# A two-layer vision kernel in fp32: y in halves, and an MLP step in another order with half-width products

## The reference

```python
# layer 0
h = depthwise_conv7x7(x) + conv_b                    # 24 channels, each by itself
h = (h - mean_c(h)) * rsqrt(var_c(h) + 1e-5) * ln_g + ln_b
h = gelu(h @ w1 + b1)                                # 24 -> 96
x = (h @ w2 + b2) * layer_scale + x                  # 96 -> 24
# layer 1
y = fc1(x) * s + t                                   # 24 -> 24
nodes = y in windows of 8 x 8                        # 64 nodes of 24 channels
idx = 9 nearest neighbours by the distance of the normalised nodes
feat = concat(node, neighbour - node)                # 9 x 48
h = max over the 9 of gelu(affine(feat @ ew))        # 48 outputs
out = affine(fc2(h)) + x
```

## Time and profile before

| | us |
|---|---|
| median of 3 runs | 2242.76 |
| lowest, highest | 2237.08, 2244.7 |
| profiled execution, its own time | 2235.85 |
| its span | 2233.8 |
| TensorE busy | 1990.3 (89%) |
| VectorE busy | 1525.1 (68%) |
| ScalarE busy | 1115.5 (50%) |
| GpSimd busy | 642.8 (29%) |
| mean granted clock of TensorE, share of 2.4 GHz | 0.934 |

### The profile page before, as it was taken

How to read it: one execution, slowest core, us unless ns; L and a number is a source line. 1 busy time by engine, 2 the same in 40 slices (tenths; PEclk the granted TensorE clock), 3 DMA queues, 4 the chain that set the end, 5 groups by cost and what they waited for, 6 DMA issues and landing times.

```text
span 2233.8 us, 45679 instructions
## 1 busy us (share of the span) xinstructions
PE 1990.3 (89%) x13970; PEld 1041.8 (47%) x13970; DVE 1525.1 (68%) x5840; ACT 1115.5 (50%) x2630; POOL 642.8 (29%) x407
## 2 busy tenths in 40 slices
PE   6998999999789888889888988888888898989986
PEld 2444555555344444444444444444444444544442
DVE  4222222222188888888788888888888797888887
ACT  0102444344356655555555555555555565655563
POOL 3002444444122222222222222322222232222232
PEclk9997999999799999999999999999899999999899
DMA  7872333333210111111111111111111111111110
GB/s 143 148 145 62 82 78 77 76 77 78 55 20 14 34 30 33 32 33 32 33 32 33 32 33 33 33 32 33 32 33 32 30 29 28 30 25 27 29 35 16
DMA packets 225814, 105.49 MB, mean 47 GB/s; under 512 B 195904, under 2 KB 222784, under 8 KB 225472
## 3 DMA queue, kind: packets, MB, share of 16 engines
q1 hardware_dynamic: 225600, 102.63, 21.8%
HBM read 54.40 MB, written 28.90 MB: 37 GB/s over the span
## 4 chain that ended last, share of the span: by engine, by line
PE 54%; issue 19%; ACT 13%; DVE 8%; POOL 5%; SPq 1%; DMA 1%; POOLq 0%; ACTq 0%; DVEq 0%
PE bank L1059 9%; PE bank L867 7%; PE bank L924 6%; PE bank L918 6%; PE bank L992 5%; ACT xam L496 4%; PE bank L1014 4%; DVE red L783 4%; PE bank L1030 3%; PE bank L892 3%; PE bank L962 2%; POOL hq L369 2%; ACT pb L512 2%; PE bank L901 2%; PE bank L955 2%
## 5 line engine op out<-in xcount | busy, mean ns | idle before, releaser
L783 DVE TENSOR_REDUCE red<-bank 128x64 f32<-128x512 f32 x1176 | 751.8, 680 | 163.8 <-PE bank L1059 145.8
L512 ACT CAST pb<-bank 64x192 bf16<-64x192 f32 x1176 | 367.3, 312 | 375.4 <-PE bank L1030 360.4
L1059 PE MATMUL bank<-onehot,pb 128*32 128x512 bf16 x7056 | 533.2, 408 | 18.5 <-issue 16.7
L369 POOL TENSOR_TENSOR hq<-red,arena 128x384 f32<-128x384 f32 x196 | 200.9, 1025 | 554.6 <-DVE red L783 539.3
L350 POOL TENSOR_TENSOR rs<-ve,mhalf 112x16 f32<-112x16 f32 x56 | 162.4, 2899 | 377.8 <-DVE ve L689 377.8
L770 DVE TENSOR_SCALAR onehot<-slot 128x256 bf16<-128x256 bf16 x1568 | 252.9, 231 | 0.0
L1059 PEld LDWEIGHTS bank<-onehot,pb 128*32 128x32 bf16 x7056 | 137.9, 98 | 207.9 <-issue 104.1
L1001 PE MATMUL bank<-arena,wqs 128*128 128x448 f32 x336 | 171.8, 595 | 42.3 <-DMA arena<-yb 38.6
L1014 PE MATMUL bank<-xb,xam 128*128 128x64 f32 x1568 | 205.8, 277 | 0.0
L1014 PEld LDWEIGHTS bank<-xb,xam 128*128 128x128 f32 x1568 | 201.8, 201 | 2.8 <-issue 2.5
L361 POOL TENSOR_TENSOR rn<-nv,mhalf 128x28 f32<-128x28 f32 x28 | 134.5, 4805 | 229.3 <-DVE nv L742 229.3
(11 more groups left out here) (92 smaller groups left out, 2719.7 us busy)
## 6 DMA issues: line engine op xcount, KB each, us to landing
arena<-yb SPq DMA_DIRECT2D x336, 56.0 KB, 2.1
arena<-in_x SPq DMA_DIRECT2D x24, 392.0 KB
ht<-conv_d SPq DMA_DIRECT2D x112, 84.0 KB
xt<-in_x SPq DMA_DIRECT2D x112, 84.0 KB
x_d<-x1o SPq DMA_DIRECT2D x112, 84.0 KB
ht<-x_d SPq DMA_DIRECT2D x112, 84.0 KB
xt<-x_d SPq DMA_DIRECT2D x56, 168.0 KB, 3.2
out<-x1o SPq DMA_DIRECT2D x112, 84.0 KB, 2.0
```

The lines of the kernel that those rows point to most:

```text
L369: nc.gpsimd.tensor_tensor(hq[:, :, :, :], red[:, k, :, :, :], qs[:, b, :, wx, :].unsqueeze(1).broadcast_to([128, 2, T, NN]), ALU.add).then ...
L512: last = nc.scalar.copy(pb[64 * u:64 * u + 64, k, part, :, :, u, :], src[64 * u:64 * u + 64, :, :, :])
L783: nc.vector.tensor_reduce(red[:, k, h, t, :], src, axis=mybir.AxisListType.X, op=op).then_inc(s["red_done"], 1)
L1059: last = mm(bank[32 * q:32 * q + 32, (k + t) % 2, :], pb[:, k, part, g, c, :, :].rearrange("p u o -> p (u o)"), onehot[:, k, g, :, :].rear ...
```

## The change

In the MLP stage:

- `variance` uses blocks of 128 pixels instead of 112, each in two halves of 64 columns of weights, 8 products instead of 4. `turn_std` follows (three blocks of 128 and one of 64). `LB` is also the partition count of `ve`, `rs` and `rse`.
- `expand` does the middle hidden block first, in two halves of output columns over all rows, and then the first and the last block in quarters of the array: rows 0 to 63 for the first, 64 to 127 for the last, each in two halves of columns. That is 6 products instead of 3.
- `contract` gives the middle block in two halves of output columns, then the first block to the lower half only and the last to the upper half only, 4 products instead of 3.
- TensorE's order for step m becomes turn_std(m+1), centre(m+4), variance(m+3), contract(m-1), expand(m). Centre is one step further ahead, and `square` on ScalarE with it, now waiting for the variance before it. gelu takes the blocks in the order middle, first, last. SyncE's and VectorE's orders stay.

In the graph stage:

- `yb` is ordered u, window, node. `load_y2` reads 448 contiguous values for each partition. `project` becomes two products, one for each half of the weights' columns.
- `fc1` of half 0 moves from window 6 to the second half of window 5, that of half 1 to the first half of window 6. `make_y` is split in two within window 6, and `square_y` comes at the end of window 6 instead of in window 0 of the next iteration. `norms` is later in VectorE's window 0, and the last `halfsq` stands before `project`.

```diff
...
 NBLK = 4
-LB = L // NBLK
+LB = 128
 NU = NI * WX
...
         outs = x1o[:, :, :].rearrange("p (b u) l -> p b u l", b=2)
-        yb = sb("yb", [128, 2, WX, 2, NN])
+        yb = sb("yb", [128, 2, 2, WX, NN])
         xa = sb("xa", [128, 2, WX, 2, NN])
...
                         g, u = (t, 3)[blk // 2], blk % 2
-                        sp.dma_start(y2[32 * blk:32 * blk + 32, b, t, :, :], yb[32 * g:32 * g + 32, b, :, u, :]
+                        sp.dma_start(y2[32 * blk:32 * blk + 32, b, t, :, :], yb[32 * g:32 * g + 32, b, u, :, :]
                                      ).then_inc(y2_in[b], 16)
             def load_res(i, b):
...
                 pool.wait_ge(s["rnt_done"], 2 * i + (k + 1))
-                nc.gpsimd.tensor_tensor(xa[:, b, lo:hi, :, :].rearrange("p w u i -> p (w u i)"),
-                                        rnt[:, lo:hi, :, :].rearrange("p w u i -> p (w u i)"),
-                                        yb[:, b, lo:hi, :, :].rearrange("p w u i -> p (w u i)"), ALU.mult
+                nc.gpsimd.tensor_tensor(xa[:, b, lo:hi, :, :], rnt[:, lo:hi, :, :],
+                                        yb[:, b, :, lo:hi, :].rearrange("p u w i -> p w u i"), ALU.mult
                                         ).then_inc(s["xa_done"], 1)
             def add_x(i, b, old, gp):
...
             def square(m, r):
                 act.wait_ge(ctr_d, m + 1)
+                at_least(act, var_d, m)
                 nc.scalar.activation(sq[:, :], bank[:, 0, 0:L], ACT.Square).then_inc(sq_d, 1)
...
             def gelu(m, r):
-                for t in range(3):
-                    act.wait_ge(mm1_d, 3 * m + (t + 1))
+                for t in (1, 0, 2):
+                    act.wait_ge(mm1_d, 3 * m + (1 if t == 1 else 3))
                     nc.scalar.activation(gl[:, t, :], bank[:, 3 + t, 0:L], ACT.Gelu, bias=b1s[:, t:t + 1], scale=1.0
...
             act.wait_ge(zeroed, 2)
-            for m in range(3):
+            for m in range(4):
                 square(m, m)
             for m in range(NBUF):
-                square(m + 3, m + 3)
+                square(m + 4, m + 4)
                 gelu(m, m)
...
                 for r in range(NBUF):
-                    square(NBUF * j + (r + 3), r + 3)
+                    square(NBUF * j + (r + 4), r + 4)
                     gelu(NBUF * j + r, r)
-            def make_y(i, b, banks=(6, 7)):
-                for u in range(2):
+            def make_y(i, b, us=(0, 1), banks=(6, 7)):
+                for u in us:
                     act.wait_ge(s["fc1_mm"], 2 * i + (u + 1))
-                    nc.scalar.activation(yb[:, b, :, u, :], bank[:, banks[u], 0:L].rearrange("p (w i) -> p w i", w=WX),
-                                         ACT.Identity, bias=c1[:, 0:1],
+                    nc.scalar.activation(yb[:, b, u, :, :].rearrange("p w i -> p (w i)"), bank[:, banks[u], 0:L], ACT.Identity, bias=c1[:, 0:1],
                                          scale=P("s1")).then_inc(s["y_done"], 1)
             def square_y(i, b):
                 act.wait_ge(s["y_done"], 2 * (i + 1))
-                nc.scalar.activation(sq2[:, :], yb[:, b, :, :, :].rearrange("p w u i -> p (w u i)"), ACT.Square
+                nc.scalar.activation(sq2[:, :].rearrange("p (w u i) -> p u w i", w=WX, u=2), yb[:, b, :, :, :], ACT.Square
                                      ).then_inc(s["ysq_done"], 1)
             def square_xa(i, b):
...
                     split(n + 1, (r + 1) % 2, 0, s["p_mm"], s["hi_done"])
-                if pre and wx == 0:
-                    square_y(i + 1, (b + 1) % 2)
+                if early and wx == 6:
+                    make_y(i + 2, b, us=(0,))
                 if ahead1:
...
                     split(n + 1, (r + 1) % 2, 2, s["res2_mm"], s["lo_done"])
+                if early and wx == 6:
+                    make_y(i + 2, b, us=(1,))
                 if pre and wx == 2:
...
                 if early and wx == 6:
-                    make_y(i + 2, b)
+                    square_y(i + 2, b)
             for m in range(NSTEP - NBUF, NSTEP):
-                if m + 3 < NSTEP:
-                    square(m + 3, m + 3)
                 gelu(m, m)
...
                     best(n - 2, r % 2, i - (wx < 2), (wx - 2) % WX, ((r - 2) % (2 * WX)) // WX, first)
-                if pre and wx == 0:
-                    norms(i + 1)
                 if pre and wx == 1:
...
                         dve.wait_ge(s["t8_done"], G * (n + 4))
+                if pre and wx == 0:
+                    norms(i + 1)
                 if gather:
...
                 for k in range(NBLK):
-                    last = mm(bank[0:LB, 2, G * k:G * k + G], sq[:, LB * k:LB * k + LB], P("mean4"), start=True, stop=True)
+                    for half in range(2):
+                        a = min(LB * k + 64 * half, L - 64)
+                        last = mm(bank[64 * half:64 * half + 64, 2, G * k:G * k + G], sq[:, a:a + 64], P("mean4"),
+                                  start=True, stop=True)
                 last.then_inc(var_d, 1)
             def turn_std(m, r):
...
                 for k in range(NBLK):
-                    last = nc.tensor.transpose(bank[:, 1, LB * k:LB * k + LB],
-                                               rse[:, r % 2, k, :, :].rearrange("p g c -> p (g c)"),
-                                               P("ident")[0:LB, 0:LB])
+                    size = min(LB, L - LB * k)
+                    last = nc.tensor.transpose(bank[:, 1, LB * k:LB * k + size],
+                                               rse[0:size, r % 2, k, :, :].rearrange("p g c -> p (g c)"),
+                                               P("ident")[0:size, 0:size])
                 last.then_inc(rb_d, 1)
             def expand(m, r):
                 pe.wait_ge(hn_d, m + 1)
-                for t in range(3):
-                    at_least(pe, gelu_d, 3 * (m - 1) + (t + 1))
-                    mm(bank[:, 3 + t, 0:L], w1g[:, t, :], hn[:, r % 2, :], start=True, stop=True).then_inc(mm1_d, 1)
+                for c in range(2):
+                    last = mm(bank[64 * c:64 * c + 64, 4, 0:L], w1g[:, 1, 64 * c:64 * c + 64], hn[:, r % 2, :],
+                              start=True, stop=True)
+                last.then_inc(mm1_d, 1)
+                for k, t in ((0, 0), (64, 2)):
+                    for c in range(2):
+                        last = mm(bank[64 * c:64 * c + 64, 3 + t, 0:L], w1g[k:k + 64, t, 64 * c:64 * c + 64],
+                                  hn[k:k + 64, r % 2, :], start=True, stop=True)
+                last.then_inc(mm1_d, 2)
             def contract(m, r):
                 at_least(pe, x1_dn, m - 1)
-                for t in range(3):
-                    pe.wait_ge(gelu_d, 3 * m + (t + 1))
-                    last = mm(bank[:, 6 + r % 2, 0:L], w2s[:, t, :], gl[:, t, :], start=t == 0, stop=t == 2)
+                for half, t in ((0, 1), (1, 1), (0, 0), (1, 2)):
+                    pe.wait_ge(gelu_d, 3 * m + (1 if t == 1 else 3))
+                    last = mm(bank[64 * half:64 * half + 64, 6 + r % 2, 0:L], w2s[:, t, 64 * half:64 * half + 64],
+                              gl[:, t, :], start=t == 1, stop=t != 1)
                 last.then_inc(mm2_d, 1)
             def mlp_slot(m, r, j, first=False):
...
                 now = m if isinstance(m, int) else 0
+                if now + 1 < end:
+                    turn_std(m + 1, r + 1)
+                if now + 4 < end:
+                    centre(m + 4, r + 4, j + (r + 4) // NBUF)
+                if now + 3 < end:
+                    variance(m + 3)
                 if not first:
                     contract(m - 1, r - 1)
-                if now + 3 < end:
-                    centre(m + 3, r + 3, j + (r + 3) // NBUF)
                 expand(m, r)
-                if now + 1 < end:
-                    turn_std(m + 1, r + 1)
-                if now + 3 < end:
-                    variance(m + 3)
...
                 variance(m)
+            centre(3, 3, 0)
             turn_std(0, 0)
...
                 at_least(pe, s["lo_done"], n)
-                both = yb[:, b, wx, :, :].rearrange("p u i -> p (u i)")
-                mm(bank[:, 3, 0:G * O], both, wp[:, :], start=True, stop=False, skip_group_check=True
-                   ).then_inc(s["p_mm"], 1)
+                for u in range(2):
+                    last = mm(bank[64 * u:64 * u + 64, 3, 0:G * O], yb[:, b, u, wx, :], wp[:, :], start=True, stop=False,
+                              skip_group_check=True)
+                last.then_inc(s["p_mm"], 1)
             def subtract(n, k, part, waits, done):
...
                 if early and wx == 6:
-                    fc1(i + 2, b, j + 1, 0)
+                    fc1(i + 2, b, j + 1, 1)
                 for e in qa:
...
                     fc2(i - 1, bn, 1)
-                if early and wx == 6:
-                    fc1(i + 2, b, j + 1, 1)
+                if early and wx == 5:
+                    fc1(i + 2, b, j + 1, 0)
```

(4 more changed lines are left out.)

## The result

The changed kernel takes 2338.64 us (median of 4 runs, 2335.68 to 2346.61) against 2241.01 for the kernel before in the same comparison: ratio 1.0442, 95% interval 1.0409 to 1.0474. The forecast was 2324, slower. The last residual of the MLP starts at 677.5 us instead of 577.1, so that stage ends 100.4 us later (forecast +100). From the end of that residual to the end of the span it is 1655.5 us instead of 1656.0 (forecast -14).

What follows compares the result with a forecast made beforehand. TensorE bounds the MLP, a TensorE-VectorE chain the graph stage; after the change SyncE's queue gates the MLP. MLP +100 (70 - 6 + 36) and graph stage -14 give +86, so 2324 us, range 2255 to 2385.

Steps and rivals of the forecast that it cites:

- Part 2: MLP stage: late ht loads in SyncE's queue make centre wait some 4 us in 24 rounds; +70 us.
- Part 3: MLP stage: waits at centre lower TensorE's clock, costing 1.5 us a round (ends 0 and 2.7), +36 us.
- Part 1: MLP step, TensorE's work: half-width products bring it from 6.65 to 5.9 us, variance at 0.85, contract at 1.7.
- case that passes start in the order written: MLP step on TensorE: contract 5u (1.9 us), expand 7 to 8u, step 6.6 to 6.7 us; u, a pass, 0.375 us.
- +100 in the MLP: MLP stage in all: +70 us for late ht loads, -6 for the other 8 steps, +36 for the low clock.
- Part 4: Graph stage, y in halves: y2 lands some 4 us sooner, its wait goes, -45 us; whole stage -14 us.
- +0.16 forecast: Graph stage, project: half-width products cost one pass more, +0.16 us to its successor (ends 0 and +0.42).
- project's 22 us: Graph stage: project's extra 0.16 us in five of seven windows, times 28, gives +22 us.
- Gate without the clock: Rival: centre waits for ht in the MLP but the clock holds; +50 us, 2289 us; chance 0.21.
- The loads keep ahead: Rival: ht comes in time, TensorE bounds the MLP at 5.9 us a step; -42 us there, 2184 us; chance 0.11.
- No overlap in fp32: Rival: halves do not overlap in the MLP, step 9.7 us, TensorE-bound; +171 us, 2397 us; chance 0.06.

Runs made afterwards that it cites:

- kept-warm run: Changed kernel plus 18 idle bf16 products of 448 columns ahead of every centre that waits for ht; 2320.5 us, ratio 1.0363.
- run with eight: Changed kernel with the MLP's old order and y2 loaded by 8 DMAs instead of 12; 2128.8 us, ratio 0.9513.
- both mended kernels: Changed kernel with ht issued ahead of the store (2188.0 us), and changed kernel with TensorE's and ScalarE's old MLP order (2172.7 us).

## Why the prediction was right, and where it was not

**The gate (Part 2), right.** The wait stands at centre, 24 times, and the loop is the one that was summed. The queue's terms held: 0.88, 8.33 (8.35), landing 2.90 (2.76). Moving the load of ht ahead in SyncE's order took it away.

**The clock (Part 3), right in kind, too small.** I took 1.5 us a round between ends of 0 and 2.7; the kept-warm run puts it at 2.6. The upper end was too low by its own rows: 0.9 for centre, 0.8 for variance and another 1.7 for a contract of twice the length are 3.4. It was not passed, as variance cost 0.4 us more and not 0.8, and centre 0.7 and not 0.9. The three products on the loop ran wholly at the low level, 5.9 us against 3.4.

**TensorE's work (Part 1), taken too dear.** The sum for the case that passes start in the order written was also wrong: with contract at 5u and expand at 7 to 8u the step is 6.7 to 7.1 us and not 6.6 to 6.7. Variance 0.49 and not 0.85; contract 1.53 and not 1.7. Eight passes in 1.53 us are 4.1 u, so halves run side by side, both passes of each, which is the 2x of the Trainium skill's "TensorEngine Tiling", Theoretical Speedup. My reading of the Trainium skill's "TensorE: Matmul & The Clock Gate", Part 3, that strict program order makes the second half wait for the first pass of its neighbour, would give 1.87 and was wrong. The drain that the Trainium skill's "TensorEngine Tiling", Key Properties, names costs at most 0.1 to 0.2 us here: the halves of expand take 0.86 and the quarters 0.91 where two whole passes take 0.75.

**+100 in the MLP, in part luck.** The round at the full clock was forecast at 16.2 and came at 15.4, of which variance and contract are 0.5; the clock was taken 1.1 too small; so 17.7 was forecast and 18.05 came. In the whole stage the gate without the clock cost +40 where +64 was forecast (MLP end of the kept-warm run), and the clock +60 where +36 was. The two errors of 24 us cancel, and that the sum fits to 0.4 us is chance. The parts, and that both are there, are not.

**y2 (Part 4), wrong.** The step that failed: "An issue takes 0.61 us now, and the store of x1, whose rows are 1792 bytes, 0.31", so that twelve, which take 8.34 us now, would take "about 4". Rows became 1792 bytes and the issue 0.59. The run with eight shows that three times the data costs 0.03 us more: among these DMAs the issue goes by their number and not by what they move. I compared DMAs that differ in more than their rows (24 partitions into DRAM against 32 partitions within SBUF). Which of these makes 0.31 or 0.59 is open; the load of x1 from DRAM, to 24 partitions too, takes 0.30, so whether DRAM is read or written is not it. The value of the wait was near: taking all but 2.3 us of it away gave 41 us (2172.7 to 2131.5), where I had put 45.

**The rest of the graph stage.** The wait of norm for square_y went as forecast (7.0 us over 15 times before, none after). In the kernel after, project starts 0.85 us behind node_terms (two passes, 0.75 before) and the gather 0.48 behind project (0.42 before), in the timeline:

```profile
1107.46 0.92 PE L1012 MATMUL bank<-arena,wqs 128*128 128x448 f32 x2
1108.31 0.55 PE L1035 MATMUL bank<-wp,yb 128*64 128x192 f32 x4
1108.79 0.83 PE L1071 MATMUL bank<-onehot,pb 128*32 128x512 bf16 x12
```

That is the +0.16 forecast, 0.10 and 0.06, but as a term of the sum it is nothing: windows 2, 3 and 4, over both iterations of a pair, last 46.4 us before and after. fc1 costs window 5 0.91 us (0.75 forecast) and gives back nothing in window 6. With y2's 45 us missing, the sum should have been about +40; it is -0.5 or, alone, -4 to -6. Besides project's 22 us, what is missing lies in window 0, which the forecast left alone but for norm. Behind the stall at the turn of TensorE's loop (once in two iterations) it lasts 11.7 us before and 9.9 after on the mean of eleven, and in the other iteration 8.6 and 8.0: some 34 us in all, 7 of them norm's. Two of the first kind before, and two after:

```profile
1192.94:1204.27 11.33, 9.52 (x68) 5.78 (x69) 5.06 (x25) 3.71 (x10) 3.84 (x1) 0.70 0.62 120
1308.91:1321.02 12.11, 10.21 (x68) 5.85 (x69) 5.05 (x24) 3.76 (x10) 3.95 (x1) 0.63 0.60 119
...
1290.83:1300.25 9.42, 9.19 (x70) 5.65 (x71) 4.20 (x19) 3.10 (x9) 3.84 (x1) 0.64 0.52 127
1406.38:1413.27 6.89, 6.38 (x70) 4.04 (x71) 4.83 (x23) 3.04 (x9) 2.94 (x1) 1.00 0.58 141
```

Most of this gain is a stall. The kernel before has two with no cause shown in each round, 23.3 us and 16.7 us over 11 times each, and the second lies in this window; the changed kernel has the first alone, 34.7 us over 11 times. It is also the window that takes the 50 us when the code is moved. So the gain, like that loss, can come from the code's place; no run tells it from the edits of the graph stage.

**The rivals.** "Gate without the clock" is the kept-warm run, and its +64 is above. "The loads keep ahead" did not happen, but it is what both mended kernels are: MLP -57, where it said -42. "No overlap in fp32" is excluded by contract's 1.53 us.

## What to carry to other kernels

When work is moved ahead by a step, look at every in-order queue that feeds it: here four DMAs stood behind a store that waits for the end of the chain which they start, and that ring, 12 us of queue and landing and 6 of products behind them, set the pace. A cheaper product pays only where its engine ends the wait last; take apart what is cheaper from what is moved, as here one gave -3.3% and the other more than took it back. A DMA's issue has a price of its own (0.59 us, and 0.62 for three times the data), so count DMAs before bytes.

## What the hardware showed that I had not expected

- The same loop on TensorE, with 54 products more ahead of it, takes 50 us more in 1656, and 44 in a second kernel, where the products stand within the MLP's code; almost all of it in one window of fourteen. In the kernel with half-width products only, whose graph stage has the instructions of the kernel before, that stage is 12 us shorter. Effects under some 2% between kernels of different code length on TensorE can be this alone.
- An fp32 product's two passes do not keep its neighbour in the other half of the array's columns from running beside both: 8 passes of 448 columns in 1.53 us, where 6 full ones take 2.25.
- The issue of a SBUF-to-SBUF DMA took 0.61 us with 224 rows of 256 bytes, 0.59 with 32 of 1792 and 0.62 with 96 of 1792.
